# A four-stage transformer block: one spread matmul per head channel in place of two, and the second group's projections issued earlier

## What is computed

```python
x = layernorm(x + L0_attn(x))     # linear attention with a decay, below
x = layernorm(x + L0_ffn(x))      # one of 8 experts, chosen by argmax(log_softmax(logits) + gumbel(u))
x = layernorm(x + L1_attn(x))     # per head: dots of projected tokens, used as weights, then a mixer
x = layernorm(x + L1_ffn(x))      # silu(x w1) * (x w2), gelu(h1), gelu(h2), w3 with ternary weights
```

```python
upd = (1.0 - k)[..., :, None] * v[..., None, :]      # per head 8 x 8
decay = k[..., :, None]
kv = scan over the tokens: kv[t] = kv[t-1] * decay[t] + upd[t]
h = einsum('nthd,nthde->nthe', q, kv).reshape(n, t, 128)
out = h @ out_w.T + out_b
```

## Time and profile before

| | |
|---|---|
| median of 3 runs | 222.52 us (221.82 to 222.86) |
| profiled execution, its own time | 223.1 us |
| its span (first to last recorded instruction) | 221.2 us |
| TensorE matmul, busy | 192.3 us, 972 instructions |
| TensorE weight load, busy | 145.2 us |
| VectorE, busy | 153.9 us |
| ScalarE, busy | 112.7 us |
| GpSimd, busy | 79.4 us |
| mean granted TensorE clock | 0.969 of full |

### The profile page before, as it was taken

How to read it: one execution, slowest core, us unless ns; L and a number is a source line. 1 busy time by engine, 2 the same in 40 slices (tenths; PEclk the granted TensorE clock), 3 DMA queues, 4 the chain that set the end, 5 groups by cost and what they waited for, 6 DMA issues and landing times.

```text
span 221.2 us, 3102 instructions
## 1 busy us (share of the span) xinstructions
PE 192.3 (87%) x972; PEld 145.2 (66%) x972; DVE 153.9 (70%) x385; ACT 112.7 (51%) x172; POOL 79.4 (36%) x67
## 2 busy tenths in 40 slices
PE   6659886978996999999999999999997989999940
PEld 6128664466873767788877868897774767666820
DVE  0378957897978679978868899777896227671143
ACT  2497923123027764322298732225996346895630
POOL 4020006121011902751345739233469332354401
PEclk9997998899999999999999999999999999999985
DMA  5995020100000010000000100000001000001001
GB/s 132 316 431 216 15 59 1 47 0 0 3 0 0 0 52 1 0 0 3 0 0 1 47 0 0 0 0 0 0 3 49 0 0 0 0 3 47 0 3 50
DMA packets 6125, 8.19 MB, mean 37 GB/s; under 512 B 480, under 2 KB 4832, under 8 KB 5728
## 3 DMA queue, kind: packets, MB, share of 16 engines
q1 hardware_dynamic: 6112, 8.02, 10.7%
HBM read 6.97 MB, written 1.05 MB: 36 GB/s over the span
## 4 chain that ended last, share of the span: by engine, by line
issue 34%; PE 23%; POOL 19%; DVE 11%; ACT 5%; DMA 4%; SPq 1%; POOLq 1%; DVEq 0%
PE c_bank L803 10%; POOL rstd L292 5%; POOL hid_even_low L308 5%; POOL hid_odd_low L308 4%; DMA xt<-x_tok 4%; POOL res L287 4%; PE y_bank L771 3%; PE b_bank L790 3%; DVE state L564 3%; DVE normed_lent L549 2%; PE b_bank L936 2%; DVE read L572 1%; ACT hid L415 1%; DVE stats L532 1%; PE b_bank L785 1%
## 5 line engine op out<-in xcount | busy, mean ns | idle before, releaser
L292 POOL TENSOR_TENSOR rstd<-varied,power 128x4 f32<-128x4 f32 x16 | 17.8, 1114 | 78.4 <-DVE varied L542 78.4
L564 DVE TENSOR_TENSOR_SCAN state<-rep_bank,keep 128x256 f32<-128x256 f32 x64 | 39.8, 670 | 4.6 <-PE rep_bank L763 4.5
L771 PEld LDWEIGHTS y_bank<-attend_pack,read 128*128 128x128 f32 x256 | 33.0, 198 | 13.2 <-DVE read L572 11.5
L771 PE MATMUL y_bank<-attend_pack,read 128*128 128x128 f32 x256 | 36.0, 287 | 5.4 <-DVE read L572 4.8
L308 POOL TENSOR_TENSOR hid_even_low<-hid,hid_even_high 128x512 fp32r<-128x512 f32 x16 | 20.4, 1283 | 34.4 <-ACT hid L415 24.8
L413 ACT ACTIVATE hid_even_high<-c_bank,scales_pack 128x512 fp32r<-128x512 f32 x16 | 11.0, 689 | 27.7 <-PE c_bank L803 27.7
L415 ACT ACTIVATE hid<-c_bank,scales_pack 128x512 f32<-128x512 f32 x32 | 21.8, 682 | 0.0
L572 DVE TENSOR_TENSOR read<-state,query 128x512 f32<-128x512 f32 x32 | 21.4, 679 | 0.0
L803 PE MATMUL c_bank<-hid_even_high,hidden_rounded 128*128 128x512 f32 x64 | 19.7, 414 | 0.6 <-ACT gate L390 0.6
L803 PE MATMUL c_bank<-hid_even_low,hidden_rounded 128*128 128x512 f32 x64 | 18.9, 400 | 0.4 <-DVE hid_even_low L595 0.4
L803 PE MATMUL c_bank<-hid_odd_high,hidden_rounded 128*128 128x512 f32 x64 | 19.2, 412 | 0.0
(11 more groups left out here) (129 smaller groups left out, 359.8 us busy)
## 6 DMA issues: line engine op xcount, KB each, us to landing
hidden_pack<-hidden SPq DMA_DIRECT2D x2, 1024.0 KB, 11.8
attend_pack<-attend SPq DMA_DIRECT2D x1, 1152.0 KB, 7.7
xT_lent<-x_chan SPq DMA_DIRECT2D x4, 256.0 KB, 8.6
xt<-x_tok SPq DMA_DIRECT2D x4, 256.0 KB, 3.2
mlp_pack<-mlp SPq DMA_DIRECT2D x1, 768.0 KB, 9.6
out<-xT_lent SPq DMA_DIRECT2D x3, 256.0 KB, 2.3
metric_pack<-metric SPq DMA_DIRECT2D x1, 384.0 KB, 13.2
project_pack<-project SPq DMA_DIRECT2D x1, 256.5 KB, 2.7
```

What stands on the lines that cost most here:

```text
L292: nc.gpsimd.tensor_tensor(rstd[n][:], varied[n][:], power[:], ALU.pow).then_inc(ln_rstd[n], 1)
L564: ins = nc.vector.tensor_tensor_scan(state[:, e % STATES, at], rep_bank[e % 2][:, at], keep[:, bass.ds(a * T + s * SEQ, SEQ)], 0.0, ALU.ad ...
L771: ins = nc.tensor.matmul(y1_bank[:, tile(j)], read[:, e % READS, tile(j)], out_w_rep_sb[:, e, :], start=(e == 0 and j == 0), stop=False, s ...
```

## The change

Values are reordered so that partition e*16 + h holds channel e of head h; the first 64 partitions are channels 0 to 3 of all heads, the last 64 channels 4 to 7. One tile (`first`) holds in its upper half the high parts of channels 0 to 3 and in its lower half their low parts; the other (`second`) holds high parts of channels 4 to 7 below and their low parts above. A 0/1 matrix with ones in both halves then spreads and adds both in one matmul. The high parts are copied by ScalarE (two instructions over 64 partitions), the low parts are subtracted by VectorE (two instructions over 64 partitions, from one half to the other). The matrices `rows_of` and `head_sum` come in a new pack `heads` of 128 KB, and ScalarE expands `rows_of` eightfold while it casts. `blocks` moves into the `metric` pack. Group 1's projections move to the middle of TensorE's and ScalarE's step one, and value differences and their parts are made one step ahead for all groups.

```diff
 PACKS = (
-    ("project", (("key_w", P), ("value_w", P), ("query_w", P), ("blocks", P), ("key_b", 1))),
-    ("attend", (("rep", HD * P), ("out_b", P), ("out_w_rep", HD * P), ("out_w", P))),
+    ("project", (("key_w", P), ("value_w", P), ("query_w", P), ("key_b", 1))),
+    ("heads", (("rows_of", HD * HEADS), ("head_sum", P))),
+    ("attend", (("out_b", P), ("out_w_rep", HD * P), ("out_w", P))),
...
@@ sync @@
                 if g == 0:
+                    load_pack("heads")
                     load_pack("scales")
                     load_pack("attend")
@@ scalar, projections() @@
-                    if n == 1:
-                        act.wait_ge(loaded["attend"], 16)
-                        nc.scalar.copy(rep_r[:], rep_sb).then_inc(rep_cast, 1)
+
+            def high_values(a):
+                act.wait_ge(dv_whole, nth(a, 1, 1))
+                if not first(a):
+                    act.wait_ge(rep_ready, nth(a, RP, 0))
+                for i in range(2):
+                    at = half(i)
+                    nc.scalar.copy(dvalue_parts[i][at, :], dvalue[at, :]).then_inc(dv_high, 1)
@@ scalar, step() @@
+                    act.wait_ge(loaded["heads"], 16)
+                    nc.scalar.copy(rep_r[:].rearrange("p e (h d) -> p e h d", h=HEADS),
+                                   rows_of_sb.unsqueeze(3).to_broadcast([P, HD, HEADS, HD])).then_inc(rep_cast, 1)
+                    act.wait_ge(const_ready, 3)
                     act.wait_ge(loaded["project"], 16)
-                    act.wait_ge(const_ready, 3)
                     projections(range(0, PROJECTIONS))
+                    high_values(a)
+                    projections(range(PROJECTIONS, 2 * PROJECTIONS))
                     act.wait_ge(loaded["scales"], 16)
                     routing()
                     round_weights()
                     for i in range(len(MLP_PACKS)):
                         sum_low_halves(i)
-                    projections(range(PROJECTIONS, 2 * PROJECTIONS))
+                    high_values(a + 1)
...
                 if first(b):
                     projections(range(3 * PROJECTIONS, NG * PROJECTIONS - 1))
+                    high_values(a + 1)
                 if c is not None:
-                    for m in range(1, NH):
+                    gelu(c, 2, 1)
+                    if a is not None:
+                        high_values(a + 1)
+                    for m in range(2, NH):
                         gelu(c, 2, m)
@@ vector @@
+            def low_values(a):
+                for i in range(2):
+                    at = half(i)
+                    dve.wait_ge(dv_high, nth(a, 2, i + 1))
+                    nc.vector.tensor_tensor(dvalue_parts[i][half(1 - i), :], dvalue[at, :],
+                                            dvalue_parts[i][at, :].bitcast(F32), ALU.subtract).then_inc(dv_ready, 1)
@@ vector, step() @@
                         dve.wait_ge(proj_out, 2)
-                    if first(b):
-                        dve.wait_ge(proj_out, 2 * PROJECTIONS)
-                    if first(a) or first(b):
                         value_steps(a)
-                    dve.wait_ge(dv_whole, nth(a, 1, 1))
-                    nc.vector.tensor_copy(dvalue_parts[0][:], dvalue[:]).then_inc(dv_high, 1)
-                    dve.wait_ge(dv_high, nth(a, 1, 1))
-                    nc.vector.tensor_tensor(dvalue_parts[1][:], dvalue[:], dvalue_parts[0][:].bitcast(F32),
-                                            ALU.subtract).then_inc(dv_ready, 1)
+                        low_values(a)
...
-                if first(b):
-                    dve.wait_ge(proj_out, 3 * PROJECTIONS - 1)
-                    value_steps(a + 1)
...
                     read_state(a, HD - 1)
-                if a is not None and c is not None:
+                if a is not None:
+                    if first(a):
+                        dve.wait_ge(proj_out, 2 * PROJECTIONS - 1)
+                    if first(b):
+                        dve.wait_ge(proj_out, 3 * PROJECTIONS - 1)
                     value_steps(a + 1)
...
                     product(b, 1)
                 if a is not None:
+                    low_values(a + 1)
                     norm_out(0, a)
@@ tensor @@
             def replicate(a, e):
-                if e == 0:
-                    pe.wait_ge(dv_ready, nth(a, 1, 1))
+                if e % (HD // 2) == 0:
+                    pe.wait_ge(dv_ready, nth(a, 2, 1 + e // (HD // 2)))
                 if not first(a) or e >= 2:
                     pe.wait_ge(scan_done, nth(a, RP, e - 1))
-                nc.tensor.matmul(rep_bank[e % 2][:], rep_r[:, e, :], dvalue_parts[0][:], start=True, stop=False)
-                nc.tensor.matmul(rep_bank[e % 2][:], rep_r[:, e, :], dvalue_parts[1][:], start=False,
+                nc.tensor.matmul(rep_bank[e % 2][:], rep_r[:, e, :], dvalue_parts[e // (HD // 2)][:], start=True,
                                  stop=True).then_inc(rep_ready, 1)
@@ tensor, step(): after replicate(a, 0) and replicate(a, 1) @@
+                if first(a):
+                    project(PROJECTIONS)
+                    project(PROJECTIONS + 1)
...
                     replicate(a, 2)
+                    if first(a):
+                        project(PROJECTIONS + 2)
+                        pe.wait_ge(loaded["attend"], 16)
                     attend(a, c, 0)
...
                     if first(a):
-                        for n in range(PROJECTIONS, 2 * PROJECTIONS):
-                            project(n)
                         pe.wait_ge(loaded["metric"], 16)
@@ host @@
+    rows_of = np.zeros((2, HD // 2, HEADS, HD, HEADS), np.float32)
+    for e in range(HD):
+        rows_of[:, e % (HD // 2), :, e, :] = np.eye(HEADS, dtype=np.float32)
```

More of the change, by code:

```diff
@@ L137, in build @@
         dvalue = sb("dvalue", [P, T])
-        dvalue_parts = [sb(f"dvalue_{which}", [P, T], F32R) for which in ("high", "low")]
+        dvalue_parts = [sb(f"dvalue_{which}", [P, T], F32R) for which in ("first", "second")]
         state = sb("state", [P, STATES, T])
@@ L218, in tile, with half @@
             return slice(j * P, (j + 1) * P)
+        def half(i):
+            return slice(i * P // 2, (i + 1) * P // 2)
         def y1_sums(a, c):
@@ L752, in sum_query @@
                     pe.wait_ge(direct_ready, a)
-                nc.tensor.matmul(proj_bank[0][:], blocks_sb, query[:, bass.ts(a, T)], start=True,
+                nc.tensor.matmul(proj_bank[0][:], head_sum_sb, query[:, bass.ts(a, T)], start=True,
                                  stop=True).then_inc(sum_ready, 1)
             def replicate(a, e):
-                if e == 0:
-                    pe.wait_ge(dv_ready, nth(a, 1, 1))
+                if e % (HD // 2) == 0:
+                    pe.wait_ge(dv_ready, nth(a, 2, 1 + e // (HD // 2)))
                 if not first(a) or e >= 2:
                     pe.wait_ge(scan_done, nth(a, RP, e - 1))
-                nc.tensor.matmul(rep_bank[e % 2][:], rep_r[:, e, :], dvalue_parts[0][:], start=True, stop=False)
-                nc.tensor.matmul(rep_bank[e % 2][:], rep_r[:, e, :], dvalue_parts[1][:], start=False,
+                nc.tensor.matmul(rep_bank[e % 2][:], rep_r[:, e, :], dvalue_parts[e // (HD // 2)][:], start=True,
                                  stop=True).then_inc(rep_ready, 1)
@@ L868, in step @@
                         project(n)
+                    pe.wait_ge(loaded["heads"], 16)
                 if c is not None:
@@ L884, in step @@
                     if first(a):
-                        pe.wait_ge(loaded["attend"], 16)
                         pe.wait_ge(rep_cast, 1)
@@ L1071 @@
         "key_b": np.asarray(L0_attn_key_b).reshape(P, 1),
-        "value_w": vq[:P].T,
+        "value_w": vq[:P][of_values].T,
         "query_w": vq[P:].T,
-        "out_w": out_t,
+        "out_w": out_t[of_values],
         "out_w_rep": out_rep,
         "out_b": rows(L0_attn_out_b),
-        "rep": rep.reshape(P, HD, P),
+        "rows_of": rows_of,
+        "head_sum": blocks[:, of_values],
         "blocks": blocks,
```

10 lines of the change are left out of this document (4 added, 6 removed).

## The result

The changed kernel takes 229.84 us (median of 4 runs, 228.86 to 230.89) against 222.69 us (4 runs) for the kernel before: ratio 1.0327, 95% interval 1.0262 to 1.0391. The forecast was 225.8 us, range 222.3 to 228.3. Its sign was right and its size was not: 7.15 us slower where 3.3 had been worked out.

What follows compares the result with a forecast made beforehand. It saw a chain of waits led in turn by TensorE, VectorE and GpSimd, not TensorE's busy time. Terms -0.7 + 0.7 + 1.3 + 1.4 + 0.1 + 0.5 = +3.3 us on a 222.52 median gave 225.8 us, range 222.3 to 228.3.

Steps and rivals of the forecast that it cites:

- the low clock: Rival, chance 0.16: new TensorE idle time in step one lowers its clock, 1 to 2 us more, 227.3 us.
- The two places of loss: VectorE idles about 2.4 us for routing() in step one; low-part subtractions ahead of norm_out(0) delay the first norm's output.
- the loop step got no shorter: Sign that the forecast is right: 32 spread instructions instead of 64, yet no loop step well under 42.5 us.
- Passes: Of 32 deleted spread matmuls only three, in steps two to four, end a scan's wait, 0.23 us each: -0.7 us.
- Start of the kernel: Step one: first scan 0.8 us earlier, but VectorE then waits 2.4 us for routing(), so scan 3 comes +0.7 us.
- H: Landing time of the new 128 KB pack at the kernel's start, taken as 6.4 us, between 5.3 and 7.0.
- The sentence on the Trainium skill: Transfers below 512 bytes miss line rate; the new pack has 1 KB a partition, so lands at 5.8: 225.2 us.
- End of step one: Low-part subtractions before norm_out(0) mostly hide in its 1.1 us wait for the inverse deviation: +0.1 us.
- End of step two: Two low-part subtractions, 1.29 us, delay norm_out(0), for which TensorE already waits: +1.3 us in full.
- Ends of steps three and four: Low-part subtractions delay norm_out(0) and TensorE's transposes, partly absorbed by VectorE's 0.83 us idle: 2 x 0.7 = +1.4 us.
- Group three's difference: Step two: moved from before scan 5's wait to behind read 7, it delays the norm sum at 61.53: +0.5 us.
- High parts on ScalarE: Two half copies of 0.58 us a group fit in ScalarE's gaps: cost 0; without that cover 1.2 a step.

Runs made afterwards that it cites:

- the run with unread matmuls: Changed kernel plus matmuls of ones that nothing reads in three of TensorE's waits, in steps one and two: 227.46 us, ratio 1.0227 to the kernel before.
- the first run: Kernel before without the second matmul of each spread pair, so the low parts are left out of the sum: 221.79 us, ratio 0.9943.
- the run with group three's difference in its old place: Changed kernel with route steps and low parts late, and group three's value difference back before scan 5 of step two: 221.85 us, ratio 0.9971.
- routing late: Changed kernel with VectorE's eight route_on steps moved behind scans 4 to 7 of step one: 227.5 us, ratio 1.0165 to the kernel before.
- late low parts: Changed kernel with low parts subtracted at the start of the group's own step, before direct; with only this edit 226.11 us, ratio 1.0096.
- The delayed kernel before: Kernel before plus two unread 64x512 subtractions ahead of norm_out(0) in steps two, three and four: 229.32 us, ratio 1.0296.
- the two single edits: Changed kernel with only the low parts moved to the start of the group's own step, 226.11 us, or only the route steps moved later, 227.5 us.
- both edits: Changed kernel with low parts at the start of the group's own step and route steps behind scans 4 to 7: 222.73 us, ratio 0.9988.
- twice the passes: Changed kernel with route steps and low parts late, each spread matmul done twice into the same bank: 223.68 us, ratio 1.0039.
- the three with matmuls in the waits: Unread matmuls of ones added to the changed kernel (227.46 us), its version with late routing, late low parts and group three's difference moved back (219.21), and the kernel before (222.83).
- The version with unread matmuls there: Changed kernel with route steps and low parts late, group three's difference before scan 5, unread matmuls in steps one and five: 219.21 us, ratio 0.9849.

## Why the prediction was right in direction and wrong in size

Two steps of the prediction failed. It let idle time of VectorE absorb half of what the low parts cost in steps three and four: these two stretches were forecast at 1.2 us net of the passes, and took 2.4. And it put the low clock behind the new waits at nothing in the sum and left it to a rival: the run with unread matmuls was 2.2 us faster than the change. An estimate from these two is 3.4 of the 3.85 us that the forecast lacked, and an upper bound, since a part of the 2.2 is low clock that the kernel before has too. The two places of loss themselves, and the small worth of the passes, were read rightly. One further sign held: the loop step got no shorter, 43.6 us from first scan to first scan where it was 42.5.

**Passes: right.** -0.7 was forecast, -1.3 and -1.1 measured, and the first run's interval, 0.4 to 2.1 us, takes in the forecast. The reading that only a pair on which a scan waits counts held: 4 waits times 0.3 us. The prediction had counted three of them and left out the one in step one.

**Start of the kernel: wrong term, and the right number by luck.** H, the landing of the new pack, was taken as 6.4. ScalarE's cast shows it:

```profile
5.34 1.04 ACT L435 CAST rep_r<-heads_pack 128x1024 fp32r<-128x1024 f32 x1 [3.11 <-DMA heads_pack<-heads]
```

It is the low end of the prediction's bounds, 5.3. By the prediction's own chain H + 13.5 is 18.8 for scan 3; it was 19.03. The chain was good, and its input off by 1.1 us. So scan 3 was 0.15 us early, not 0.7 late; that +0.7 stands at the first norm's sum after all is the work of the low clock behind it, which the term did not hold. This is one execution: over the eight kernels with this pack the cast started between 5.02 and 6.05, and in six of them the first scan started near 12.1 and not at 11.41. In the run with group three's difference in its old place the cast started at 5.09, and keys waited 0.85 us for TensorE behind it, so the pack does not always set the start. The sentence on the Trainium skill ("DMA: Bandwidth & Descriptors", Specifications) had given 5.8: the nearer value. But the trace does not bear out the reason: the small pack, with its rows of 160 bytes as before, now took 3.4 us and not 5.3; in the kernels with the old order it took anything from 3.9 to 5.4.

**End of step one: +0.1 was +0.8.** The pair was to hide in the norm's wait for the inverse deviation. That wait became longer, because GpSimd's instruction did:

```profile
34.66 1.52 POOL L299 TENSOR_TENSOR rstd<-varied,power 128x4 f32<-128x4 f32 x1 [21.59 <-DVE varied L563]
```

It ran beside the two subtractions (34.62 to 36.0). The first norm's in step one took 1.52 us in each of the three kernels profiled that have low parts there, and 1.02 or 1.03 in the nine others. With routing late, at clocks alike (0.66 and 0.69 over 36 to 41 us), this stretch is 0.5 us longer with early low parts than with late ones. With late low parts the stretch is still 0.4 us longer than before, at a clock of 0.50 in one run and 0.69 in the other. At full clock, though, the changed kernel and the kernel before pass it in the same time within 0.1 us (both with unread matmuls: -0.96 and -1.03 to before). So the +0.8 comes about half with the early pair and half without it, and all of it only where the clock is low; how the two work together is not shown. The Trainium skill ("GPSIMD Engine Reference", 1. Specifications) says that GpSimd's SBUF interfaces are shared with VectorE, with contention from VectorE instructions that have two inputs in SBUF. These subtractions are such instructions, and the two durations agree with it; no run changed their kind, so the port itself is not shown.

**End of step two: +1.3 was 1.7 and more.** The pair took 1.43 us and not 1.29: the starts lie 0.71 apart, where the two of the earlier trace rows lie 0.6 apart. With the clock held full the stretch cost 1.7, the gain of a pass already taken off; the low clock behind the 2.67 us wait added 0.5.

**Ends of steps three and four: the first step that failed.** I let 0.83 us of VectorE's idle before product 0 absorb a part of the pair, and had 0.7 left. The end of step three in the changed kernel, VectorE, then TensorE, then ScalarE:

```profile
116.89 0.69 DVE L583 TENSOR_TENSOR dvalue_first<-dvalue,dvalue_first 64x512 fp32r<-64x512 f32 x1
117.60 0.69 DVE L583 TENSOR_TENSOR dvalue_second<-dvalue,dvalue_second 64x512 fp32r<-64x512 f32 x1
118.33 1.11 DVE L570 TENSOR_SCALAR normed<-total,moments,rstd 128x128 f32<-128x128 f32 x4
119.35 0.75 DVE L607 SCALAR_TENSOR_TENSOR hid<-rep_bank,scales_pack,gate 128x512 f32<-128x512 f32 x1
```

```profile
118.72 1.10 PE L808 MATMUL b_bank<-metric_pack,normed 128*128 128x128 f32 x4 [0.85 <-DVE normed L570]
```

```profile
119.86 0.59 ACT L397 COPY x1T<-b_bank 128x512 f32<-128x512 f32 x1 [1.19 <-PE b_bank L808]
120.83 0.69 ACT L402 ACTIVATE gate<-c_bank,scales_pack 128x512 f32<-128x512 f32 x1 [0.38 <-PE c_bank L826]
```

Product 0 (119.35) did swallow its idle. It came 4.50 us later than before, hardly more than the 3.91 by which the step had started late. But product 0 was not what the rest waited for. The norm's output came 5.42 us later, so TensorE's transposes waited 0.85 us where they had waited for nothing; the matmuls behind them, x1T's copy, the second gate and product 1 are all some 5.1 to 5.3 later, 1.2 to 1.4 more than the step's start. That chain (output, transposes, copy, gate, product 1) stood in the prediction; the error was to take VectorE's idle time ahead of product 0 off it, which is not on that chain. The pairs of steps three and four cost 1.0 and 1.3 us in all, after the gain of the passes. The delayed kernel before, which has no such gain, lost 1.3 and 1.4, twice the 0.7 of the prediction.

The pair at the end of step four serves nothing: there are four groups, and with a = 3 `low_values(a + 1)` makes the parts of a fifth. The change runs five pairs, the versions with late low parts four. So the 1.3 us of that place could be had back by leaving the pair out there; no run tests that alone.

**The clock, the second: a rival where it should have been a term.** It was held apart with chance 0.16, at step one alone, 1 to 2 us. The rows show the clock low behind the new waits, at 20 to 25 and 75 to 80 us, and in step five. Behind the waits of 0.85 us in steps three and four it stayed at 1.00 (118 to 124 and 162 to 168 us). The Trainium skill ("TensorE: Matmul & The Clock Gate", What's actually happening) says that throttled is the default and activity releases it; the rows agree, in that the run with matmuls in the waits has 1.00 in all these stretches and is 2.2 us faster. The forecast waits of over 2 us, in step one and at the end of step two, should have carried a price for it: 0.86 and 0.5 us by the run with the clock held. Step five is the place that I did not see at all: no edit lies there. TensorE waits there for the second norm in pieces of 0.89 us, before and after alike. Behind that the clock fell somewhere between 171 and 183 us in the profiled execution of the change and of five other kernels: the passes alone, each of the two single edits, the delayed kernel, and both edits with group three's difference moved back. It did not fall in that of before, of both edits, of twice the passes, or of any of the three with matmuls in the waits. The change's own four runs, 228.86 and 229.11 us at clock 0.957 and 0.958, 230.56 and 230.89 at 0.942, have a step of the same size. That suggests a matter of the execution and not of the kernel; each kernel was profiled once, so it is not shown, and what decides it stays open.

**Group three's difference: right.** +0.5 forecast, 0.5 by the profiles with both edits and with the difference moved back, too little for the times to tell.

**High parts on ScalarE: free by the trace.** They take 0.61 us each, and behind the pair of step three ScalarE still waits 3.03 us for TensorE. No run takes them out, so they are not ruled out as a part of what the version with both edits still loses.

## What to carry to other kernels

A deleted instruction is worth its length times the number of waits that end on it, read from the table of waits, and not times its count. A new instruction put ahead of a norm's output is on the path of everyone who waits for that output: follow that chain (here the transposes), and don't credit idle time of another chain on the same engine. Where an edit makes TensorE wait anew for long (2.6 us and more here), add a price for low clock behind the wait. Try unread matmuls in it once the waits themselves are as short as they can be: here they gained 1.2% then, 1.0% in the changed kernel and nothing in the kernel before.

## What the runs showed of the hardware

- An instruction over 64 partitions cost as much as one over 128: VectorE's subtraction 0.69 us, like the 0.69 of a 128x512 one, ScalarE's copy 0.61 against 0.58 for the query's. Reading one half and writing the other cost nothing more.
- The same subtraction took 1.65 us in step two when it stood at the start of the step (over 128 partitions in the kernel before, over 64 with late low parts), while GpSimd added a residual, and 0.69 in step three.
- The pack of 128 KB landed 3.6 us after its issue (3.3 to 4.3 over the eight kernels that have it); the pack of 20.5 KB behind it took 3.4 (3.1 to 4.1), where it took 5.3 in the kernel before and 3.9 to 5.4 over the four kernels with that order. So its size and its rows alone do not set that figure.
- A 128x4 instruction of GpSimd took 1.52 us beside two subtractions of VectorE, and 1.02 or 1.03 at the same place without them. In each of steps three and four two such instructions took 1.40 and 1.42, in the kernel before and in the change alike; in the change VectorE had one product or subtraction of two SBUF tiles beside each.
- The granted clock fell in a stretch of step five that no edit touches, in six of the twelve executions profiled; from the second norm's sum to the third's that step was then 1.4 to 1.6 us longer. The version with unread matmuls there has the narrowest times of all that ran more than four times (218.99 to 220.46).
